# Two decoder layers on one core: routing in five groups, and four steps of the first layer's rotation in other places

## The reference

```
x = x + scan(norm(x))          # L0: 16 sequential steps; each takes a gradient step on W1, b1, W2, b2
x = x + xattn(norm(x), ctx)    # L0: 16 heads, 77 keys, output product and bias bo
x = x + experts(norm(x))       # L0: top 2 of 8 experts
x = x + attn(norm(x))          # L1: 16 heads of self attention with a slope bias
x = x + xattn(norm(x), ctx)    # L1: cross attention, masked, no output product; the values have a bias bv
x = x + experts(norm(x))       # L1: top 2 of 8
```

## Time and profile before

| | us |
|---|---|
| median of 3 runs | 727.4 (725.42 to 727.99) |
| the profiled execution | 721.61 |
| its span | 719.5 |
| first rotation, from 61.6 to the first load of rows | 208 |
| experts 0, to about 358 | 89 |
| second rotation, to about 616 | 258 |
| experts 1, to the end | 103 |

### The profile page before, as it was taken

How to read it: one execution, slowest core, us unless ns; L and a number is a source line. 1 busy time by engine, 2 the same in 40 slices (tenths; PEclk the granted TensorE clock), 3 DMA queues, 4 the chain that set the end, 5 groups by cost and what they waited for, 6 DMA issues and landing times.

```text
span 719.5 us, 18483 instructions
## 1 busy us (share of the span) xinstructions
PE 568.0 (79%) x6160; PEld 461.8 (64%) x6160; DVE 484.0 (67%) x1361; ACT 429.5 (60%) x897; POOL 361.8 (50%) x646
## 2 busy tenths in 40 slices
PE   3796999998997508999479999987897761699970
PEld 1485777776875408999447676755675550699960
DVE  6653468878777534555359999875998875355536
ACT  1452378886784325888246767664885652488840
POOL 5711434555588763565453434223446767256550
PEclk9897579998899857999869999998999995699995
DMA  7749980000000012222460000000000001222215
GB/s 196 222 148 335 338 267 2 2 3 1 10 16 25 27 48 67 72 72 61 123 280 3 2 3 1 3 1 2 2 3 17 25 27 49 60 72 67 67 40 170
DMA packets 42089, 52.66 MB, mean 73 GB/s; under 512 B 11197, under 2 KB 37133, under 8 KB 41709
## 3 DMA queue, kind: packets, MB, share of 16 engines
q1 hardware_dynamic: 33229, 40.04, 17.9%
q0 software_dynamic: 4544, 9.35, 3.9%
q10 hardware_dynamic: 4224, 2.10, 1.0%
HBM read 41.04 MB, written 28.22 MB: 96 GB/s over the span
## 4 chain that ended last, share of the span: by engine, by line
issue 69%; PE 11%; POOL 6%; DVE 2%; DMA 2%; SPq 1%; POOLq 0%; DVEq 0%; ACTq 0%
PE p_s L1682 5%; POOL yo L1584 5%; PE p_o L1692 3%; PE p_in L1692 2%; DVE x L1635 2%; POOL to_row L1579 1%; PE p_pT L1674 1%; DMA yo<-context,to_row 1%; SPq L288 1%; DMA back<-yo 0%; DMA context<-xs 0%; SPq L1711 0%; SPq L1707 0%; SPq L1715 0%; DVE context L1618 0%
## 5 line engine op out<-in xcount | busy, mean ns | idle before, releaser
L1584 POOL DMA_INDIRECT yo<-context,to_row x78 | 76.0, 975 | 68.7 <-DVE context L1618 33.7
L1642 ACT ACTIVATE context<-pack 128x1156 f32 x78 | 90.6, 1166 | 31.2 <-DVE context L1618 13.4
L1682 PE MATMUL p_s<-xT_f,context 128*128 128x128 f32 x624 | 85.9, 283 | 0.0
L1682 PEld LDWEIGHTS p_s<-xT_f,context 128*128 128x128 f32 x624 | 79.3, 199 | 0.0
L1123 POOL DMA_INDIRECT xs<-send,x_index x64 | 64.1, 1001 | 23.3 <-issue 17.0
L1611 DVE TENSOR_SCALAR context<-p_s,context 128x128 f32<-128x128 f32 x156 | 47.4, 345 | 28.9 <-PE p_s L1682 23.9
L1317 ACT ACTIVATE x_pT<-p_pT 128x512 f32<-128x512 f32 (+1 forms) x96 | 48.8, 525 | 23.6 <-PE p_pT L1424 21.8
L1649 ACT ACTIVATE context<-p_s,context 128x128 f32<-128x128 f32 x156 | 47.6, 356 | 21.7 <-PE p_s L1682 12.6
L1424 PE MATMUL p_pT<-sq,x_prob 128*128 128x128 f32 x320 | 52.9, 291 | 4.8 <-ACT x_pT L1317 3.1
L1159 DVE TENSOR_REDUCE x_top<-p_s 128x12 f32<-128x924 f32 (+2 forms) x48 | 46.9, 1005 | 10.4 <-PE p_s L1410 10.4
L1309 ACT ACTIVATE x_prob<-x_prob 128x1024 f32<-128x1024 f32 x64 | 42.8, 717 | 12.7 <-DVE x_prob L1169 11.7
(11 more groups left out here) (255 smaller groups left out, 1486.2 us busy)
## 6 DMA issues: line engine op xcount, KB each, us to landing
xs<-in_blank SPq DMA_DIRECT2D x2, 8707.5 KB, 42.5
pack<-in_pack SPq DMA_DIRECT2D x16, 578.0 KB, 9.1
context<-xs SPq DMA_DIRECT2D x78, 64.5 KB
back<-yo SPq DMA_DIRECT2D x8, 256.0 KB, 4.8
back<-yo ACTq DMA_DIRECT2D x8, 256.0 KB, 5.4
yo<-context,to_row POOLq DMA_INDIRECT x78
x<-in_x SPq DMA_DIRECT2D x4, 256.0 KB, 4.7
xs<-send,x_index POOLq DMA_INDIRECT x64
```

Source lines behind the costliest of these rows:

```text
L1584: nc.gpsimd.indirect_dma_start(yo[:, :], bass.IndirectOffsetOnAxis(to_row[:, n % NY, :], 0), y[:, n % NY, :], None).then_inc(y_stored[n % ...
L1642: nc.scalar.activation(ws[:, n % NW, :], pack[:, bass.ds(e, 1), :].rearrange("p a w -> p (a w)"), ACT.Copy).then_inc(ws_ready, 1)
L1682: ins = mm(p_h[n % 2][k // 2][:, P * (k % 2):P * (k % 2 + 1)], ws[:, n % NW, P * k:P * (k + 1)], xT[:, n % 2, :], start=True, stop=True)
```

## The change

1. `GROUPS` becomes 5, 5, 2, 2, 2: one more `choose`, `rank` and `address` in each of x0 and x1, for the batches 10 and 11.
2. `SCATTER_ROUND` becomes a written list. Before it is 11, 12, 13, 14, 15, 16, 17, 18, 19, then 20 five times, 22, 22. Now the batches 5 and 6 go in one round, 8 and 9 in one, 10 and 11 in one, 12 and 13 in one.
3. In the first rotation POOL does `slope1` ahead of the row norm. PE's `rturn` and ACT's `c_rturn` move behind the scan's gradient and the copy of the queries, with their waits.
4. For the batches 9 to 15 of x0 the row norm is DVE's, at the head of its round (`late_route_norm`).
5. In x1 the bias is a second product into `po_out` and no longer an addition on POOL.

```diff
-GROUPS = (5, 5, 4, 2)
+GROUPS = (5, 5, 2, 2, 2)
...
+SCATTER_ROUND = [11, 12, 13, 14, 15, 16, 16, 17, 18, 18, 19, 19, 20, 20, 22, 22]
...
-FIRST_POOL = ((2, "rstd"), (2, "norm"), (0, "slope0"), (7, "rnorm"), (0, "slope1"), (9, "scat"), (2, "kT"), (6, "rrstd"))
+FIRST_POOL = ((2, "rstd"), (2, "norm"), (0, "slope0"), (0, "slope1"), (7, "rnorm"), (9, "scat"), (2, "kT"), (6, "rrstd"))
...
+LATE = NB - 7
...
         def route_norm_in_pool(b, p):
+            if b >= LATE:
+                return
...
-        return [(SCATTER_ROUND, scatter), ({at: at - 1 for at in range(NB + LAG)}, joint_rstds), (0, masked_k), (2, add_bias)]
+        return [(SCATTER_ROUND, scatter), ({at: at - 1 for at in range(NB + LAG)}, joint_rstds), (0, masked_k)]
...
         def residual(b, p):
             dve.wait_ge(projected_o, FIRST + b + 1)
-            if not beside:
+            if own:
                 dve.wait_ge(biased, b + 1)
...
+        def late_route_norm(b, p):
+            if b < LATE:
+                return
+            dve.wait_ge(r_in_pool, 2 * (b + 1))
+            nc.vector.tensor_scalar(send[:, b, :, 1:], x[:, b, :].unsqueeze(1).to_broadcast([P, 2, P]), r_mv[:, b, 0:1], r_rstd[:, b:b + 1],
+                                    ALU.subtract, ALU.mult).then_inc(r_normed, 1)
...
         def project(b, p):
             pe.wait_ge(turned_sb, FIRST + b + 1)
             if q is not None:
-                wait(pe, xr_sb, FIRST + b - LAG + 1)
+                wait(pe, xr_sb, FIRST + b - LAG + (0 if beside else 1))
...
             if name == "x1":
-                mm(po_out, oT, eye, start=True, stop=True).then_inc(projected_o, 1)
+                mm(po_out, oT, eye, start=True, stop=False)
+                mm(po_out, m["first_row"], m["bo_x1"][:, :], start=False, stop=True).then_inc(projected_o, 1)
...
         def route_turn(b, p):
             pe.wait_ge(r_normed, FIRST + b + 1)
             if beside:
-                pe.wait_ge(turned_sb, min(b + LAG + 1, NB))
+                pe.wait_ge(q_sb, min(b + LAG + 1, NB))
```

More of the change, by code:

```diff
@@ L98, in staggered @@
                     stage(b, b % 2)
-def scatter_rounds():
-    rounds = []
-    for b in range(NB):
-        known = min(e for e in GROUP_END if e >= b) + 7
-        rounds.append(max(known, rounds[-1] + 1 if rounds and known < NB + 4 else known))
-    return rounds
-SCATTER_ROUND = scatter_rounds()
+SCATTER_ROUND = [11, 12, 13, 14, 15, 16, 16, 17, 18, 18, 19, 19, 20, 20, 22, 22]
 FIRST_PE = ((3, "score"), (0, "aT"), (1, "aq"), (0, "a"), (4, "tp0"), (5, "po"), (0, "eT"), (2, "turn_in"), (1, "gw2"), (4, "tp1"), (1,
-    "out"), (0, "e_"), (7, "rturn"), (0, "dh"), (4, "tp2"), (8, "rank"), (2, "project"), (0, "g2"), (0, "g1"), (4, "mix"), (0, "g1b"), (7,
+    "out"), (0, "e_"), (0, "dh"), (4, "tp2"), (8, "rank"), (2, "project"), (0, "g2"), (0, "g1"), (7, "rturn"), (4, "mix"), (0, "g1b"), (7,
     "rlogit"))
-FIRST_DVE = ((5, "scale"), (8, "choose"), (3, "max"), (0, "eTa"), (5, "res"), (1, "w2n"), (0, "slope2"), (0, "slope3"), (1, "comb"), (0,
+FIRST_DVE = ((7, "late_rnorm"), (5, "scale"), (8, "choose"), (3, "max"), (0, "eTa"), (5, "res"), (1, "w2n"), (0, "slope2"), (0, "slope3"), (1, "comb"), (0,
     "da"), (8, "address"), (3, "shift"), (1, "count"), (0, "w1n"), (5, "rcount"), (0, "b1n"), (0, "w2Tn"))
-FIRST_ACT = ((0, "hT"), (1, "hq"), (0, "acopy"), (4, "pT0"), (2, "c_turn"), (0, "h"), (4, "pT1"), (0, "e"), (7, "c_rturn"), (4, "pT2"), (2,
-    "c_q"), (3, "exp"), (7, "c_rlg"))
-FIRST_POOL = ((2, "rstd"), (2, "norm"), (0, "slope0"), (7, "rnorm"), (0, "slope1"), (9, "scat"), (2, "kT"), (6, "rrstd"))
+FIRST_ACT = ((0, "hT"), (1, "hq"), (0, "acopy"), (4, "pT0"), (2, "c_turn"), (0, "h"), (4, "pT1"), (0, "e"), (4, "pT2"), (2, "c_q"), (7,
+    "c_rturn"), (3, "exp"), (7, "c_rlg"))
+FIRST_POOL = ((2, "rstd"), (2, "norm"), (0, "slope0"), (0, "slope1"), (7, "rnorm"), (9, "scat"), (2, "kT"), (6, "rrstd"))
 def rotation(table, stages):
@@ L1241, in vector @@
         if beside:
-            return dict(count=count_x, scale=scale_out, max=find_top, shift=shift, res=residual, rcount=route_count, choose=choose, address=address)
+            return dict(count=count_x, scale=scale_out, max=find_top, shift=shift, res=residual, rcount=route_count, choose=choose, address=address,
+                        late_rnorm=late_route_norm)
         if own:
```

## The result

The changed kernel was slower: 730.47 us (median of 20 runs) against 725.95 us (20 runs of the kernel before on the same chip), a ratio of 1.0077 with the interval 1.0051 to 1.0103. Forecast were 723.6 us, a gain of 0.5%. The profiled execution has a span of 725.2 us against 719.5, so the pair of traces shows about the difference of the medians (5.7 against 4.5 us); both executions are among the shorter ones of their kernels. On another chip the sign was the opposite; this came out in the experiments and is told there.

The account below looks back on a forecast made before the run. ACT's closing chain was taken to bound the scan's rounds and POOL's scatter queue the ends of x0 and x1. The sum -3.5 - 0.3 = -3.8 us on the median 727.4 gave 723.6 us, 8-in-10 range 716 to 729.

Parts of the forecast that it names:

- slope1 ahead of the row norm: Scan rounds: 9.25 us instead of 9.65, ACT's closing chain starting later; sum -2.0 us, between +1 and -11.
- The loss of 2.4 us a round: Scan rounds: with the skill's 1380 ns drain per table switch a round would be 12.0 us; not counted.
- Transposition in rounds 16 to 18: Behind the query product with no scan to hide it: +1.3 us, from 0 to +2.5.
- Row norm on VectorE: Batches 9 to 15 of x0: 0.54 us each, +0.1 net; POOL is freed of 10 us.
- Third choice: Round 19 of x0: 3.06 us with its rank wait, uses up all lead, +0.4; in x1 about 2.5 us of room.
- the last addresses come at 257.8: End of x0: 256.42 plus 0.4 for the choice, 0.9 for the transposition, 0.1 for the norm.
- The lower clock: PE falling to half clock in its wait of round 19 would cost another 1.4 us; not in the sum.
- -3.5 for x0: Start of experts 0: only four scatters follow the last addresses, ending at 263.0 instead of 266.5.
- x1's -0.3: End of x1, bound by POOL's stream: 612.3 against 612.7, so -0.3 us, from -2.5 to +2.5.
- The bias by a product: x1: at most 16 x 0.28 us on PE, hidden in its idle time; 0, up to +1.
- C: Rival, chance 0.13: POOL waits for late third addresses at scatters ahead of batch 15's row statistics; +5, 732 us.
- A: Rival, chance 0.18: the slope's wait comes back in full in the scan; about -9, 718 us.

Follow-up runs that it names:

- e15: Kernel before with only two batches' scatters in single rounds (18 and 20 of x0, likewise x1), the same code as e4 on another chip: ratio 1.0017.
- e16: Kernel before with parts 1 and 2 of the change (groups 5, 5, 2, 2, 2 and the new scatter rounds): ratio 0.9991.
- e17: Kernel before with the groups 5, 5, 2, 2, 2 alone, scatter rounds of before: ratio 1.0076.
- e1: Kernel before with part 3 alone (slope1 ahead of the row norm, row transposition moved behind): 723.09 against 726.84 us, ratio 0.9952.
- e18: The same code as e1 (part 3 alone, in the kernel before) on another chip: ratio 1.0014.
- e12: Kernel before with part 4 alone (row norm of batches 9 to 15 of x0 by VectorE): ratio 1.0018.
- e13: The changed kernel itself, run again on another chip: 712.77 against 719.72 us for the kernel before, ratio 0.9905.
- e6: Changed kernel with the scatter rounds of before, groups 5, 5, 2, 2, 2 kept: ratio to the kernel before 1.0062.
- e11: Kernel of e1 with the bias of x1 by a product as well (parts 3 and 5): ratio to the kernel before 1.0003.
- upper row: Chips where the kernel before took 725 to 727 us, latest completions beside scatters 2.3 to 3.6 us; lower row: 719.4 to 719.9 us, 0.14 us.
- e5: Changed kernel, POOL waiting from batch 5 on for the same round's mix ahead of a batch's scatters: ratio to the kernel before 1.0385.
- e7: Kernel of e1 with POOL waiting from batch 5 on for the same round's mix ahead of scatters: ratio to the kernel before 1.0271.
- e8: Kernel of e7, in x1 waiting ahead of every batch's scatters, joint row statistics moved ahead of them: ratio to the kernel before 1.0479.
- e10: Kernel of e1, POOL waiting from batch 5 on for the mix one round earlier ahead of scatters: ratio to the kernel before 1.0104.
- e4: Kernel before with only two batches' scatters in single rounds (18 and 20 of x0, likewise x1), groups 5, 5, 4, 2: ratio 1.0093.

## Why the prediction was wrong

- *slope1 ahead of the row norm*: the mechanism was right (ACT closes the round, with the copy ahead of the load), the size was off: 0.82 a round and not 0.40, since the gradient is out 3.96 and not 4.27 after the Gelu. The rounds 8 to 11 are 8.84 us in most traces with the new order; in a few, one of them is 1.5 us longer. From the Gelu of round 7 to that of round 15 the changed kernel gained 6.3 us (82.2 to 75.9), where the term was -2.0, inside its bounds. The part from the rounds 12 to 14, 2.5 us, can't be read from one pair: round 12 in the old order takes 11.7 us in e15, 14.1 before and 15.5 in e16 and e17, at a granted clock of 1.00, 0.79 and 0.72 from 166 to 190 us. The loss of 2.4 us a round that the prediction works out for a drain compares a round with drains to one without, so it was no price of the edit.
- *Transposition in rounds 16 to 18*: from residual 11 to 15, +1.3 was 2.0 in e1 against before (31.2 and 29.2 us) and 1.4 in e18 against e15 (34.4 and 33.0), which has the same mixes at the lower clock. The term and its range hold. What it left out is that the mixes themselves can fall to the lower clock.
- *Row norm on VectorE*: 0.41 and not 0.54 us each, +0.1 stands (e12). What the Trainium skill says of VectorE and GpSimd locking each other out (SBUF — State Buffer, Who interferes with whom) does not show with this instruction: its seven instances take 405 to 437 ns, the one wholly beside a scatter 0.41 us, and that scatter 0.96 as others. Whether it ran in a two-port mode the trace doesn't tell.
- *Third choice*: its 3.06 us are there. In e17, where nothing is late, the kernel loses 5 us with it. I let POOL's queue cover it, and POOL waited for addresses instead.
- **The step that failed** is "the last addresses come at 257.8". I moved the scatters on POOL's list only and gave them no price on another engine. In its terms: the overlap of scatters and mix stood at 0, and two mixes at the lower clock were not in the sum. In this trace the mixes beside four scatters were complete 2.92 and 3.57 us late, and the mix of batch 15 started at 246.82 where I had 242.3. The row for it was in the trace of before: the reciprocal at 231.40, "remote", 1.69 behind the mix. I had not asked what held it. The late completions are 5.0 us of this, by e13. The lower clock is the other term: the prediction prices it at 1.4 in round 19 and leaves it out of the sum, and here it took two mixes more than before, 1.3 us each, and stretched the products around them. With the third choice they outweighed the lead of 5.6 us at residual 12, which was larger than forecast. The bursts alone are not the whole: without them (e6) the kernel still loses 0.6%. The last addresses came at 264.2, and -3.5 for x0 became +2.9; x1's -0.3 became +1.8 (5.8 less the 4.0 at its second addresses); 1.1 came between the two.
- *A reading that was wrong*: at 256.42, when the last addresses were out, not eight scatters of the third group and two of batch 9 were still queued, but four of the third group and the four of the last two batches. The eight start here:

```profile
256.69 0.96 POOL L1123 DMA_INDIRECT xs<-send,x_index  x1 [0.31 <-issue]
```

- *The bias by a product*: e11 against e18 (1.0003 and 1.0014, on two chips) shows no cost.
- *The rivals*: C gave 732 us and a slower kernel, but not by its mechanism. POOL did not wait for the third addresses: it waited 7.2 us for the row statistics of batch 14 and sent the batches 10 and 11 behind them. The scan's rounds of 8.84 us lie between the forecast (9.25) and A (8.4). A had the sign on one chip, but its mechanism, a full return, is not there; that e13 gained more than forecast is no merit of the prediction.

Where completions are not late (e13), the kernel gains 7 us, more than the 3.8 forecast. Slope alone and groups with rounds alone gain nothing on those chips (1.0014, 0.9991). That they need each other, the one for the lead and the other for a queue that lets it through, fits e18 (14 scatters in a row up to 270.28) and e13 (4, up to 266.07), but it is argued and not shown; e18's lower clock is a rival to it.

Open: what makes a completion late, and why in the groups of the upper row and not in those of the lower. The runs show that it needs scatters beside the mix (e5, e7 and e8) and that it differs by chip or by group; they do not show the way. Open is also when the lower clock comes. e1 has one of the mixes of the rounds 17 and 18 at it and e18, the same code on another chip, both; what decides, no run shows.

## What to carry to other kernels

A wait that the profile puts down to nothing it knows can be the price of something that runs beside it, as here: find what, before you schedule twice as much of it there. A wait is a poor tool to move work on an in-order engine, since all that stands behind it moves too (e5, e7 to e10). A change near 1% is to be timed on more than one chip: here the sign was another on the next. Before a round of one trace is compared with that of another, compare their granted clocks: round 12 of the same order took from 11.7 to 15.5 us.

## What was not expected of the hardware

- The completion of a chain of 48 products came 0.4 to 3.6 us after its recorded end with indirect scatters beside it on the chips of the upper row, and 0.05 to 0.14 us after it on those of the lower, in the same code.
- At the end of x0 before, PE's single products were not held, though scatters followed each other from 249.00 to the end: the logits of PE ended at 250.53 and ACT's copy started at 250.57, the next logits at 252.29 and 252.33.
- In e4 PE itself stood 2.73 us between two pieces of its scores, until the fourth scatter had ended; in e15, the same code on another chip, it did not stand.
- VectorE's norm of 128x256 took 0.41 us, POOL's of the same shape 1.23 us, each beside other work.
